# Attention queries kept in DRAM by chunk: one load a chunk, two stores a batch

## The chip, the cores and the metric

The kernel runs on one core of one Trainium2 chip. The metric is the device time of one execution in microseconds.

## What is computed

Two layers over x of shape (8, 512, 256), each an attention and a feed-forward block with a residual and a layer norm behind each. The change is in the attention of the second layer, which mixes the 16 heads of one token with each other, token by token:

```python
xn = _rms(x, g1)
Q, K, V = ...            # xn @ W.T, each (b, s, H=16, HD=16)
pQ, pK = elu(Q), elu(K)
Q1, Q2 = split(pQ, 2, axis=-1);  K1, K2 = split(pK, 2, axis=-1)
kv1 = einsum('bshe,bshd->bsed', K1, V) * SCALE
kv2 = einsum('bshe,bshd->bsed', K2, V) * SCALE
lmb = exp(lp[0] * lp[1]) - exp(lp[2] * lp[3]) + LAMBDA_INIT
attn = einsum('bshe,bsed->bshd', Q1, kv1) - lmb * einsum('bshe,bsed->bshd', Q2, kv2)
```

So components 0 to 7 of a head's query are scaled by SCALE and components 8 to 15 by -lmb * SCALE. Before that come the first layer (a retention block and a ternary feed-forward block), after it norms per head and per row, an MLP, routing, and eight experts.

## The kernel before

Everything is f32; the 4096 tokens are 32 tiles of 128. The kernel has three programs behind one another: first layer and projections, attention with MLP and routing, experts. In each, every engine runs its own list of instructions and waits on semaphores; SP issues nearly all DMAs from one list, in order.

**Projections** (end of the first program, `attention_inputs`). A batch is 512 tokens. For each of 8 batches the matmul engine transposes the normalised tokens (`front`, L1338) and makes six items: two of queries (L1365), two of keys and two of values (`interleaved`, L1349). ScalarE takes exp and relu of an item (L1297, L1298), VectorE joins them to an elu (L1418) and writes the result into `res[b % 2]`, queries with the scale `qscale` (L1424). `qscale` is a column that differs between the first and the second half of each group of 16 partitions, made by five small steps (L1433 to L1442) just before the first normalisation of this stage (L1403). SP stores each batch: the queries with one DMA (L1266), the keys and values with two each (L1270). Before VectorE writes `res[b % 2]` again, it waits on `stored[n][b % 2]`.

The query tensor in DRAM is (256 features, 4096 tokens), so a store moves rows of 512 tokens (2 KB). After batch 2 SP also issues the loads of chunk 0, after batch 4 the queries and keys of chunk 1.

**Attention** (`attention_mlp_and_route`). A unit is 8 tiles, a chunk m is one half (64 tokens) of each of the 8 tiles of a unit, and there are 8 chunks. The queries of a chunk are brought to 128 partitions (tile j times component e) with 16 heads and 64 tokens in each:

```python
for j in range(GROUPS):      # 8
    src = net.q_dram.rearrange("(h e) t -> e h t", e=HD)[:, :, first:first + HALF]
    sp.dma_start(net.q[m % 2][j * HD:(j + 1) * HD, :, :], src)
```

that is 8 DMAs of 64 KB in runs of 64 tokens (256 B). Keys and values go to a ring of three buffers, 8 DMAs each, with runs of 1 KB. The matmul engine runs rounds n of 16 columns each, four rounds a chunk: `scores(n)` (L1687), `mix(n - 2)` (L1710), `turn_scores(n - 1)` (L1696), `turn_mixes(n - 3)` (L1718), and in some rounds `turn_heads` (L1726). The first `scores` of a chunk waits for the queries (`q_in`) and the keys (`ring_in`), and each `scores` for a bank (`a_taken`); the first `mix` of a chunk waits for its values, each for `t_taken` (the copy at L2023). SP's list in this loop is, for each chunk m from 2 on: wait until the scores of chunk m - 2 are done (`a_made`), queries of m; wait until the mixes of chunk m - 2 are done (`o_made`), keys of m; wait until the scores of chunk m - 1 are done, values of m. VectorE makes the copies of each round and, between them, the norms of heads and rows (L2036 to L2087).

Of the kernel before, what the change touches and what calls it, by code (L numbers as in the profile page):

```python
# [6 lines left out]
F32 = mybir.dt.float32  # L7
# [8 lines left out]
P = 128  # L16
# [34 lines left out]
def constant_table(names, of_them):  # L51
# [25 lines left out]

    parts["firsthalf"] = (p % HD < HD // 2).astype(np.float64)[:, None]
    parts["sums"] = np.stack([(p // 32 % 2 == k) / (32.0 * HID) for k in range(2)], 1)
# [74 lines left out]
class Net:  # L154


    def __init__(self, nc, ctx, args):
# [11 lines left out]

        self.q_dram = nc.dram_tensor("q_dram", [DIM, TOKENS], F32).ap()  # L170
        self.kv_dram = nc.dram_tensor("kv_dram", [2, ROWS4, TOKENS * RUN], F32).ap()
# [1044 lines left out]

STORES = (16, 32, 32)


def attention_inputs(net, ctx):  # L1220
# [24 lines left out]

    res = [[spare[:, (3 * p + n) * KD * SEQ:(3 * p + n + 1) * KD * SEQ].rearrange("p (k t) -> p k t", k=KD) for n in range(3)] for p in two]
    bank = [ph.ps(f"bank{i}", [P, SEQ]) for i in range(8)]
    pE, pV, pX = [bank[i] for i in (1, 2, 0, 3)], bank[4:6], bank[6:8]
# [11 lines left out]
    def sync(sp):  # L1260
        for b in range(BATCH):
            for n in range(3):
                sp.wait_ge(item_ready.sem, item_ready.after(ITEMS * b + KD * (n + 1)))
                kept = stored[n][b % 2].sem
                if n == 0:
                    sp.dma_start(net.q_dram[:, b * SEQ:(b + 1) * SEQ].rearrange("(k p) t -> p k t", p=P), res[b % 2][0]).then_inc(kept, 16)  # L1266
                else:
                    tokens = net.kv_dram[n - 1, :, b * SEQ * RUN:(b + 1) * SEQ * RUN].rearrange("r (j h c) -> h r j c", j=KD, h=2)
                    for h in two:
                        sp.dma_start(tokens[h], res[b % 2][n][h * ROWS4:(h + 1) * ROWS4, :, :]).then_inc(kept, 16)  # L1270
            if b in (2, 4):

                for n in range(3):
                    for kept in stored[n]:
                        sp.wait_ge(kept.sem, kept.after(STORES[n] * b // 2))
            if b == 2:
                sp.wait_ge(net.ring_zeroed.sem, net.ring_zeroed.after(4 * RING))
                load_queries(net, sp, 0)
                load_keys(net, sp, 0)
                load_values(net, sp, 0)  # L1280
            if b == 4:
                load_queries(net, sp, 1)
                load_keys(net, sp, 1)
# [103 lines left out]
    def vector(dve):  # L1387
# [18 lines left out]
        def body(b, p, before, behind, between=None):  # L1406
            if behind:
                norm(b + 1, 1 - p)
            for n in range(ITEMS):
# [13 lines left out]
                if part == 0:  # L1423
                    ins = dve.tensor_scalar(to, rl[n % 2][:, :], 1.0, qscale[:, :], ALU.subtract, ALU.mult)  # L1424
                elif part == 1:
                    ins = dve.tensor_scalar(to, rl[n % 2][:, :], 1.0, None, ALU.subtract)
                else:
                    ins = dve.tensor_copy(to, pV[n - 4][:, :])
                ins.then_inc(item_ready.sem, 1)

        def first(last_norm):
            dve.wait_ge(exp_lam.sem, exp_lam.after(1))
            dve.tensor_tensor(lmb[:, 0:1], lmb[:, 2:3], lmb[:, 3:4], ALU.subtract).then_inc(steps.sem, 1)  # L1433
            dve.wait_ge(steps.sem, steps.done(1))
            dve.tensor_scalar(lmb[:, 0:1], lmb[:, 0:1], LAMBDA_INIT, 1.0, ALU.add, ALU.add).then_inc(steps.sem, 1)
            dve.wait_ge(steps.sem, steps.done(1))

            dve.tensor_scalar(lmb[:, 1:2], net.table["firsthalf"], lmb[:, 0:1], 1.0, ALU.mult, ALU.add).then_inc(steps.sem, 1)
            dve.wait_ge(steps.sem, steps.done(1))
            dve.tensor_tensor(lmb[:, 1:2], lmb[:, 1:2], lmb[:, 0:1], ALU.subtract).then_inc(steps.sem, 1)  # L1440
            dve.wait_ge(steps.sem, steps.done(1))
            dve.tensor_scalar(qscale[:, :], lmb[:, 1:2], RET_SCALE, None, ALU.mult).then_inc(steps.sem, 1)  # L1442
            dve.wait_ge(steps.sem, steps.done(1))
# [50 lines left out]
def load_queries(net, sp, m):  # L1494
    for j in range(GROUPS):
        first = (m // 2 * GROUPS + j) * P + m % 2 * HALF
        src = net.q_dram.rearrange("(h e) t -> e h t", e=HD)[:, :, first:first + HALF]
        sp.dma_start(net.q[m % 2][j * HD:(j + 1) * HD, :, :], src).then_inc(net.q_in[m % 2].sem, 16)

# [18 lines left out]
def attention_mlp_and_route(net, ctx):  # L1518
# [157 lines left out]
    def _(pe):  # L1676
        def scores(n):

            m = n // SETS
            if n % SETS == 0:  # L1680
                pe.wait_ge(net.q_in[m % 2].sem, net.q_in[m % 2].after(128 * (m // 2 + 1)))
                pe.wait_ge(net.ring_in[2 * m % RING].sem, net.ring_in[2 * m % RING].after(128 * (2 * m // RING + 1)))
# [1017 lines left out]
def laid_out(inputs):  # L2700
# [4 lines left out]
    wk = given("L1_attn_Wk").reshape(split, RUN, HD, DIM).transpose(1, 0, 2, 3).reshape(DIM, DIM)  # L2705
    wv = given("L1_attn_Wv").reshape(HD, split, RUN, DIM).transpose(2, 1, 0, 3).reshape(DIM, DIM)
    column = lambda v: v.reshape(-1, P).T
    every = lambda v: np.broadcast_to(v.reshape(1, -1), (P, v.size))
# [6 lines left out]
        "w_fcT": flat(given("L0_ffn_W_fc").T), "w_projT": flat(given("L0_ffn_W_proj").T),  # L2715
        "w_qkvT": by_rows(np.concatenate([given("L1_attn_Wq"), wk, wv], 0).T),
        "w_1T": by_rows(given("L1_attn_W1").T), "w_2T": by_rows(given("L1_attn_W2").T),
# [18 lines left out]
```

## Time and profile before

| | |
|---|---|
| median of 3 runs | 923.56 us (922.23 to 925.37) |
| span of the profiled execution | 923.6 us |
| granted TensorE clock, mean | 0.953 |
| DVE, ACT, POOL busy | 67%, 52%, 28% |
| q1 (the hardware queues of SP) | 71376 packets, 72.36 MB, 25.5% of 16 engines |
| packets under 512 B | 22592 |

The profile is of one execution; nothing that can be measured lies between its span and the time of the runs. Times in the rows are microseconds from the start of the span. Of a matmul row with a gap before it the bracket gives the idle time and what ended it; "issue" means that the profile shows no releaser. The projection stage lasts from about 412 to 515 us, the attention loop from 518 to 633 us. PEclk is the granted clock as a share of full speed.

### The profile page before, as it was taken

Reading aid. Unit: us, or ns where it says so; the run is one execution under the profiler, and the core shown is the slowest. Engines: PE = TensorE matmul, PEld = TensorE weight load, DVE = VectorE, ACT = ScalarE, POOL = GpSimd, SP = SyncE. Lnnn points to the kernel's source line nnn. Section 1 sums busy time; section 2 is a strip of 40 time slices with the busy share of each in tenths; the row PEclk is TensorE's granted clock in tenths of the full one; section 3 lists DMA queues with packets and bytes.
Section 4 is the critical chain, followed back from the end, with each engine's and each line's share of the span. In section 5 each row is a group of like instructions: output and inputs, shape, how many; then the busy total and the mean of one; then the engine's idle time right before and its main releaser. Section 6 shows DMA issues by size and latency. Waiting matters only on the chain. (4 is left out here: it accounts for less than half of the span.)

```text
span 923.6 us, 23206 instructions
## 1 busy us (share of the span) xinstructions
PE 826.7 (90%) x8838; PEld 688.1 (75%) x8838; DVE 614.9 (67%) x1408; ACT 481.8 (52%) x999; POOL 254.6 (28%) x323
## 2 busy tenths in 40 slices
PE   5999999998899999998999889889989839999960
PEld 4788888887677777766777778777667729999960
DVE  2578787878547777777565425677776875756626
ACT  2444444443777777766954324544654224445325
POOL 1156664221202222223000000004232131656344
PEclk9999999999999999999999989999989769999985
DMA  8500000000000000002476344435222212656439
GB/s 309 184 25 17 23 17 23 17 11 2 1 1 1 1 2 1 1 1 70 139 194 189 99 111 114 117 89 178 92 93 92 92 29 84 161 160 190 122 50 344
DMA packets 76429, 79.56 MB, mean 86 GB/s; under 512 B 22592, under 2 KB 66496, under 8 KB 75968
## 3 DMA queue, kind: packets, MB, share of 16 engines
q1 hardware_dynamic: 71376, 72.36, 25.5%
q0 software_dynamic: 3968, 5.25, 3.3%
q8 instruction: 50, 0.82, 0.4%
q10 hardware_dynamic: 1008, 0.91, 0.3%
q14 instruction: 27, 0.22, 0.1%
HBM read 50.71 MB, written 27.79 MB: 85 GB/s over the span
## 5 line engine op out<-in xcount | busy, mean ns | idle before, releaser
L713 DVE TENSOR_TENSOR r_prob<-r_pS,const 128x512 f32<-128x512 f32 x128 | 82.0, 682 | 25.1 <-PE r_pS L540 25.1
L1089 DVE SCALAR_TENSOR_TENSOR f_gl<-att_res,small_first,f_gh 128x512 fp32r<-128x512 f32 x64 | 47.3, 748 | 37.2 <-ACT f_gh L1014 34.7
L943 PE MATMUL f_pY<-wpjT,f_gh 128*128 128x256 f32 x256 | 66.1, 292 | 0.3 <-DVE f_gl L1089 0.3
L944 PE MATMUL f_pY<-wpjT,f_gl 128*128 128x256 f32 x256 | 63.4, 281 | 0.0
L1349 PEld LDWEIGHTS q_bank<-q_xT,att_res 128*64 128x64 f32 x1024 | 55.6, 137 | 7.2 <-issue 4.2
L943 PEld LDWEIGHTS f_pY<-wpjT,f_gh 128*128 128x128 f32 x256 | 48.7, 190 | 15.9 <-issue 13.4
L2426 POOL DMA_INDIRECT sum_dram<-e_yo,y_id x24 | 43.1, 1795 | 63.1 <-ACT e_yo L2559 47.4
L1349 PE MATMUL q_bank<-q_xT,att_res 128*64 128x128 f32 x1024 | 59.2, 274 | 0.0
L1008 ACT ACTIVATE att_res<-f_pH 128x512 f32<-128x512 f32 x64 | 38.0, 594 | 40.1 <-PE f_pH L928 39.4
L2540 ACT ACTIVATE e_hh<-e_pH 128x320 fp32r<-128x320 f32 x64 | 26.2, 433 | 55.3 <-PE e_pH L2465 55.0
L839 POOL TENSOR_SCALAR t_ey<-t_es 128x8 f32<-128x8 f32 x4 | 0.8, 202 | 195.0 <-ACT t_sqrow L1911 195.0
L928 PE MATMUL f_pH<-f_xh,wfcT 128*128 128x512 f32 x128 | 52.4, 409 | 0.0
L928 PE MATMUL f_pH<-f_xl,wfcT 128*128 128x512 f32 x128 | 51.1, 399 | 0.0
L944 PEld LDWEIGHTS f_pY<-wpjT,f_gl 128*128 128x128 f32 x256 | 48.7, 190 | 1.8
L1014 ACT ACTIVATE f_gh<-att_res,small_first 128x512 fp32r<-128x512 f32 x64 | 46.3, 723 | 2.1
L2599 DVE SCALAR_TENSOR_TENSOR e_hl<-e_pH,e_hh 128x320 fp32r<-128x320 f32 x64 | 28.5, 486 | 28.3 <-ACT e_hh L2540 28.3
L2023 DVE COPY t_scT<-t_pT 128x256 f32<-128x256 f32 x32 | 14.0, 438 | 48.1 <-PE t_pT L1696 47.0
L512 PE MATMUL r_pQV<-r_xT,w_first 128*128 128x128 f32 x256 | 37.2, 292 | 9.7 <-DMA r_xT<-xT 7.3
L1687 PE MATMUL t_pA<-t_ring,t_q 128*16 128x128 f32 x1024 | 36.7, 284 | 7.9 <-issue 4.5
L1418 DVE SCALAR_TENSOR_TENSOR q_rl<-q_ex,q_rl 128x512 f32<-128x512 f32 x32 | 22.1, 691 | 29.6 <-ACT q_rl L1298 29.3
L512 PEld LDWEIGHTS r_pQV<-r_xT,w_first 128*128 128x128 f32 x256 | 33.4, 204 | 10.8 <-DMA w_first<-w_qkv 7.2
L1710 PE MATMUL t_pO<-t_ring,t_scT 128*16 128x128 f32 x1024 | 36.0, 280 | 4.9 <-DVE t_scT L2023 4.8
(307 smaller groups left out, 2363.2 us busy)
## 6 DMA issues: line engine op xcount, KB each, us to landing
kv_dram<-att_res SPq DMA_DIRECT2D x32, 256.0 KB, 3.7
t_ring<-kv_dram SPq DMA_DIRECT2D x128, 64.0 KB, 2.3
wi<-L_ffn_wi SPq DMA_DIRECT2D x8, 1024.0 KB
wo<-L_ffn_wo SPq DMA_DIRECT2D x8, 1024.0 KB
x_res<-L_attn_x SPq DMA_DIRECT2D x8, 512.0 KB, 5.1
q_dram<-att_res SPq DMA_DIRECT2D x8, 512.0 KB, 3.1
t_q<-q_dram SPq DMA_DIRECT2D x64, 64.0 KB, 2.8
x_dram<-x_res SPq DMA_DIRECT2D x8, 512.0 KB, 3.0
```

The costliest lines, as they stand in the source:

```text
L512: pe.matmul(pQ[:, m, :], w[:, k, m * P:(m + 1) * P], xT[t][:, k, :], start=(k == 0), stop=(k == KD - 1))
L713: dve.tensor_tensor(prob[t % 2][:, r, :, :], pS[r][:, :, :], dec[:, r, :, :], ALU.mult)\
L928: mm = pe.matmul(pH[c % 2][:, :], net.wfcT[:, k, c * P:(c + 1) * P], part[b % 2][:, k, :], start=(k == 0 and part is xh), stop=(k == KD - ...
L943: pe.matmul(out, gh[c % 4][:, cols], net.wpjT[:, c, :], start=(c == 0 and t % 2 == 0), stop=False, skip_group_check=True)
L944: mm = pe.matmul(out, gl[c % 4][:, cols], net.wpjT[:, c, :], start=False, stop=(c == NH - 1), skip_group_check=True)
L1008: nc.scalar.activation(g[c][:, :], pH[c % 2][:, :], ACT.Gelu).then_inc(gelued.sem, 1)
L1014: nc.scalar.activation(gh[c % 4][:, :], g[c][:, :], ACT.Copy, scale=net.lnw[:, c:c + 1]).then_inc(high.sem, 1)
L1089: dve.scalar_tensor_tensor(out=gl[c % 4][:, :], in0=g[c][:, :], scalar=net.lnw[:, c:c + 1], in1=gh[c % 4][:, :], op0=ALU.mult, op1=ALU.sub ...
L1349: mm = pe.matmul(to, net.wqkvT[:, k, cols], xT[p][:, k, tile], start=(k == 0), stop=(k == KD - 1))
L1687: mm = pe.matmul(pA[n % 2][32 * c:32 * c + HEADS, g, :], net.q[m % 2][:, :, at], net.ring[2 * m % RING][:, :, at * RUN:(at + 1) * RUN], st ...
L1710: mm = pe.matmul(pO[n % 2][32 * c:32 * c + HEADS, g, :], scT[n % 2][:, 4 * g + c, :], net.ring[i % RING][:, :, at * RUN:(at + 1) * RUN], s ...
L2426: pool.indirect_dma_start(net.sum_dram[:, :], bass.IndirectOffsetOnAxis(ap=net.y_id[0:n, r, e:e + 1], axis=0), yo[e % 2][0:n, r, :], None, ...
```

## The change

The query tensor in DRAM becomes (8 chunks, 2048 rows, 64 tokens), the 2048 rows being (tile, component, head). A chunk is then one block of 512 KB in which each partition of the loaded tile has one run of 4 KB, and one DMA loads it. The rows of the query weights are reordered on the host to (component, head), so that the first item of the projection holds components 0 to 7 of all heads and the second 8 to 15. The scale becomes a constant for the first and one value (-lmb * SCALE on every partition) for the second item, which takes three steps out of its making. VectorE writes the queries as (tile, item, token), 128 tokens a run. A store of a batch's queries becomes two DMAs, one for each half of the tiles, with runs of 64 tokens (256 B). `STORES` and the count that the matmul engine waits for follow.

```diff
--- before.py
+++ after.py
@@ -75,7 +75,6 @@
 
     parts["first"] = np.tile(EXPERTS - np.arange(EXPERTS), (P, 1))
 
-    parts["firsthalf"] = (p % HD < HD // 2).astype(np.float64)[:, None]
     parts["sums"] = np.stack([(p // 32 % 2 == k) / (32.0 * HID) for k in range(2)], 1)
     parts["rmseps"] = np.full((P, 1), RMS_EPS)
     parts["minushalf"] = np.full((P, HEADS), -0.5)
@@ -167,7 +166,7 @@
         self.w2T = self.sb("w2T", [P, KD, DIM])
 
 
-        self.q_dram = nc.dram_tensor("q_dram", [DIM, TOKENS], F32).ap()
+        self.q_dram = nc.dram_tensor("q_dram", [2 * UNITS, GROUPS * DIM, HALF], F32).ap()
         self.kv_dram = nc.dram_tensor("kv_dram", [2, ROWS4, TOKENS * RUN], F32).ap()
         self.x_dram = nc.dram_tensor("x_dram", [TOKENS, DIM], F32).ap()
         self.sum_dram = nc.dram_tensor("sum_dram", [TOKENS, DIM], F32).ap()
@@ -1214,7 +1213,7 @@
 
 
 
-STORES = (16, 32, 32)
+STORES = (32, 32, 32)
 
 
 def attention_inputs(net, ctx):
@@ -1244,6 +1243,11 @@
     rl = [ph.sb(f"rl{i}", [P, SEQ]) for i in two]
 
     res = [[spare[:, (3 * p + n) * KD * SEQ:(3 * p + n + 1) * KD * SEQ].rearrange("p (k t) -> p k t", k=KD) for n in range(3)] for p in two]
+
+    def queries_of(p):
+
+        return res[p][0].rearrange("p k t -> p (k t)").rearrange("p (a t) -> p a t", t=P)
+
     bank = [ph.ps(f"bank{i}", [P, SEQ]) for i in range(8)]
     pE, pV, pX = [bank[i] for i in (1, 2, 0, 3)], bank[4:6], bank[6:8]
     lam_ready, exp_lam = (ph.sig(n) for n in ("lam_ready", "exp_lam"))
@@ -1263,7 +1267,10 @@
                 sp.wait_ge(item_ready.sem, item_ready.after(ITEMS * b + KD * (n + 1)))
                 kept = stored[n][b % 2].sem
                 if n == 0:
-                    sp.dma_start(net.q_dram[:, b * SEQ:(b + 1) * SEQ].rearrange("(k p) t -> p k t", p=P), res[b % 2][0]).then_inc(kept, 16)
+                    tiles = queries_of(b % 2)
+                    for half in two:
+                        rows = net.q_dram[b // 2 * 2 + half].rearrange("(b a p) t -> b p a t", b=2, p=P)[b % 2]
+                        sp.dma_start(rows, tiles[:, :, half * HALF:(half + 1) * HALF]).then_inc(kept, 16)
                 else:
                     tokens = net.kv_dram[n - 1, :, b * SEQ * RUN:(b + 1) * SEQ * RUN].rearrange("r (j h c) -> h r j c", j=KD, h=2)
                     for h in two:
@@ -1421,7 +1428,9 @@
                 else:
                     dve.wait_ge(v_made.sem, v_made.after(2 * b + n - 4 + 1))
                 if part == 0:
-                    ins = dve.tensor_scalar(to, rl[n % 2][:, :], 1.0, qscale[:, :], ALU.subtract, ALU.mult)
+                    to = queries_of(p).rearrange("p (t k) c -> p t k c", k=KD)[:, :, n, :]
+                    elu = rl[n % 2][:, :].rearrange("p (t c) -> p t c", c=P)
+                    ins = dve.tensor_scalar(to, elu, 1.0, qscale[:, :] if n else RET_SCALE, ALU.subtract, ALU.mult)
                 elif part == 1:
                     ins = dve.tensor_scalar(to, rl[n % 2][:, :], 1.0, None, ALU.subtract)
                 else:
@@ -1432,14 +1441,7 @@
             dve.wait_ge(exp_lam.sem, exp_lam.after(1))
             dve.tensor_tensor(lmb[:, 0:1], lmb[:, 2:3], lmb[:, 3:4], ALU.subtract).then_inc(steps.sem, 1)
             dve.wait_ge(steps.sem, steps.done(1))
-            dve.tensor_scalar(lmb[:, 0:1], lmb[:, 0:1], LAMBDA_INIT, 1.0, ALU.add, ALU.add).then_inc(steps.sem, 1)
-            dve.wait_ge(steps.sem, steps.done(1))
-
-            dve.tensor_scalar(lmb[:, 1:2], net.table["firsthalf"], lmb[:, 0:1], 1.0, ALU.mult, ALU.add).then_inc(steps.sem, 1)
-            dve.wait_ge(steps.sem, steps.done(1))
-            dve.tensor_tensor(lmb[:, 1:2], lmb[:, 1:2], lmb[:, 0:1], ALU.subtract).then_inc(steps.sem, 1)
-            dve.wait_ge(steps.sem, steps.done(1))
-            dve.tensor_scalar(qscale[:, :], lmb[:, 1:2], RET_SCALE, None, ALU.mult).then_inc(steps.sem, 1)
+            dve.tensor_scalar(qscale[:, :], lmb[:, 0:1], LAMBDA_INIT, -RET_SCALE, ALU.add, ALU.mult).then_inc(steps.sem, 1)
             dve.wait_ge(steps.sem, steps.done(1))
             batches(dve, body, steps, 4, first=last_norm)
 
@@ -1492,10 +1494,8 @@
 
 
 def load_queries(net, sp, m):
-    for j in range(GROUPS):
-        first = (m // 2 * GROUPS + j) * P + m % 2 * HALF
-        src = net.q_dram.rearrange("(h e) t -> e h t", e=HD)[:, :, first:first + HALF]
-        sp.dma_start(net.q[m % 2][j * HD:(j + 1) * HD, :, :], src).then_inc(net.q_in[m % 2].sem, 16)
+    src = net.q_dram[m].rearrange("(p h) t -> p h t", h=HEADS)
+    sp.dma_start(net.q[m % 2][:, :, :], src).then_inc(net.q_in[m % 2].sem, 16)
 
 
 def load_diagonal(net, sp, part, m, i):
@@ -1678,7 +1678,7 @@
 
             m = n // SETS
             if n % SETS == 0:
-                pe.wait_ge(net.q_in[m % 2].sem, net.q_in[m % 2].after(128 * (m // 2 + 1)))
+                pe.wait_ge(net.q_in[m % 2].sem, net.q_in[m % 2].after(16 * (m // 2 + 1)))
                 pe.wait_ge(net.ring_in[2 * m % RING].sem, net.ring_in[2 * m % RING].after(128 * (2 * m // RING + 1)))
             pe.wait_ge(a_taken.sem, a_taken.after(n - 1))
             for g in range(4):
@@ -2704,6 +2704,7 @@
     split = HEADS // RUN
     wk = given("L1_attn_Wk").reshape(split, RUN, HD, DIM).transpose(1, 0, 2, 3).reshape(DIM, DIM)
     wv = given("L1_attn_Wv").reshape(HD, split, RUN, DIM).transpose(2, 1, 0, 3).reshape(DIM, DIM)
+    wq = given("L1_attn_Wq").reshape(HEADS, HD, DIM).transpose(1, 0, 2).reshape(DIM, DIM)
     column = lambda v: v.reshape(-1, P).T
     every = lambda v: np.broadcast_to(v.reshape(1, -1), (P, v.size))
     by_head = lambda v: np.repeat(v.reshape(KD, HPK).T, HD, 0)
@@ -2713,7 +2714,7 @@
         "xT": x.reshape(TILES, P, KD, P).transpose(0, 3, 2, 1),
         "w_qkv": by_rows(given("L0_attn_W_qkv")),
         "w_fcT": flat(given("L0_ffn_W_fc").T), "w_projT": flat(given("L0_ffn_W_proj").T),
-        "w_qkvT": by_rows(np.concatenate([given("L1_attn_Wq"), wk, wv], 0).T),
+        "w_qkvT": by_rows(np.concatenate([wq, wk, wv], 0).T),
         "w_1T": by_rows(given("L1_attn_W1").T), "w_2T": by_rows(given("L1_attn_W2").T),
         "small": np.concatenate([column(given("L1_attn_g1")), every(given("L1_attn_lambda_params")), flat(given("L1_ffn_w_router")),
                                  every(given("L1_attn_g2")), every(given("L1_attn_g3"))], 1),
```

## Rows read from the trace of the kernel before

**Rows 1.** The page: busy time of each engine, and one group of instructions.
```profile
PE 826.7 (90%) x8838; PEld 688.1 (75%) x8838; DVE 614.9 (67%) x1408; ACT 481.8 (52%) x999; POOL 254.6 (28%) x323
...
L1418 DVE SCALAR_TENSOR_TENSOR q_rl<-q_ex,q_rl 128x512 f32<-128x512 f32 x32 | 22.1, 691 | 29.6 <-ACT q_rl L1298 29.3
```

**Rows 2.** The page: DMA issues, count, KB each, median us to landing.
```profile
kv_dram<-att_res SPq DMA_DIRECT2D x32, 256.0 KB, 3.7
t_ring<-kv_dram SPq DMA_DIRECT2D x128, 64.0 KB, 2.3
...
q_dram<-att_res SPq DMA_DIRECT2D x8, 512.0 KB, 3.1
t_q<-q_dram SPq DMA_DIRECT2D x64, 64.0 KB, 2.8
```

**Rows 3.** Timeline of TensorE, attention loop: start, us, instruction, idle before it.
```profile
529.14 1.12 PE L1687 MATMUL t_pA<-t_ring,t_q 128*16 128x128 f32 x32
530.06 1.08 PE L1710 MATMUL t_pO<-t_ring,t_scT 128*16 128x128 f32 x32
...
535.08 1.12 PE L1687 MATMUL t_pA<-t_ring,t_q 128*16 128x128 f32 x32
...
541.21 1.95 PE L1687 MATMUL t_pA<-t_ring,t_q 128*16 128x128 f32 x32 [3.11 <-issue]
...
546.69 1.20 PE L1687 MATMUL t_pA<-t_ring,t_q 128*16 128x128 f32 x32
...
569.77 1.12 PE L1687 MATMUL t_pA<-t_ring,t_q 128*16 128x128 f32 x32 [0.51 <-issue]
...
598.34 1.13 PE L1687 MATMUL t_pA<-t_ring,t_q 128*16 128x128 f32 x32 [0.89 <-issue]
...
611.36 1.54 PE L1710 MATMUL t_pO<-t_ring,t_scT 128*16 128x128 f32 x32 [3.06 <-DVE t_scT L2023]
```

**Rows 4.** Timeline of SP's DMA queue: start, us of issuing, instruction, count.
```profile
427.14 0.39 SPq L1266 DMA_DIRECT2D q_dram<-att_res  x1
...
529.43 4.90 SPq L1498 DMA_DIRECT2D t_q<-q_dram  x8
534.38 8.61 SPq L1507 DMA_DIRECT2D t_ring<-kv_dram  x16
...
548.81 8.90 SPq L1507 DMA_DIRECT2D t_ring<-kv_dram  x16
557.96 4.88 SPq L1498 DMA_DIRECT2D t_q<-q_dram  x8
...
586.98 4.44 SPq L1498 DMA_DIRECT2D t_q<-q_dram  x8
591.46 9.95 SPq L1507 DMA_DIRECT2D t_ring<-kv_dram  x16
```

**Rows 5.** Windows: busy us by engine, granted clock, DMA share, GB/s.
```profile
498.00:510.00 12.00, 12.00 (x150) 9.30 (x148) 6.04 (x11) 5.59 (x11) 0.00 (x0) 1.00 0.48 141
524.40:529.40 5.00, 5.00 (x120) 4.24 (x112) 1.58 (x4) 2.39 (x4) 0.00 (x0) 1.00 0.32 83
529.43:534.30 4.87, 4.87 (x138) 4.28 (x129) 1.55 (x3) 1.93 (x4) 0.00 (x0) 1.00 0.44 103
541.20:543.00 1.80, 1.79 (x36) 1.80 (x40) 0.00 (x0) 0.00 (x0) 0.00 (x0) 0.50 0.48 138
```

**Rows 6.** Timeline of VectorE, projection stage.
```profile
423.10 0.21 DVE L1438 TENSOR_SCALAR q_lmb<-const,q_lmb 128x1 f32<-128x1 f32 x1
...
423.73 1.14 DVE L1403 TENSOR_SCALAR q_xn<-x_res,q_rs 128x256 f32<-128x256 f32 x4
...
438.37 0.49 DVE L1424 TENSOR_SCALAR att_res<-q_rl,q_qscale 128x512 f32<-128x512 f32 x1
...
507.93 0.49 DVE L1424 TENSOR_SCALAR att_res<-q_rl,q_qscale 128x512 f32<-128x512 f32 x1
```

**Rows 7.** Timeline of TensorE, projection stage.
```profile
424.93 1.09 PE L1338 MATMUL q_bank<-const,q_xn 128*128 128x128 f32 x8 [2.74 <-DVE q_xn L1403]
```

## The prediction, made before the changed kernel was run

> **What bounds the kernel now.** I read the page's busy shares first: the matmul engine is busy 90% of the span [rows 1], so what the change can give back must be idle time of that engine, or work at its lower clock, on the way to the end. Second, the page's DMA issues: 64 loads `t_q<-q_dram` of 64 KB beside 128 of the key and value ring, and 8 stores of queries [rows 2]. Third, the timeline of the matmul engine over the attention loop (518 to 631 us): it runs without a gap except at a few starts of a round. Those at 541.21, 569.77 and 598.34 begin with `scores` of chunks 2, 4 and 6 and are put down to "issue", that is to nothing the profile names; `scores` waits there only for the chunk's queries and keys and for `a_taken`. The other large one (611.36, 3.06 us) waits for VectorE's copy at L2023 and has nothing to do with loads [rows 3].
>
> Fourth, SP's queue in the same stretch. It works without rest: 8 query loads take 4.4 to 4.9 us of issuing, 16 ring loads 8.6 to 10 us [rows 4], some 13.5 to 15 us a chunk, where four rounds of the matmul engine at 2.97 us (529.14 to 535.08 is two) take 11.9. Take chunk 2. Its keys may be issued when `mix(3)` is done, at 530.06 + 1.08 = 531.14, but SP is then still issuing queries (529.43 to 534.33) and starts the keys at 534.38. Eight of them take half of 8.61, 4.3 us, and land 2.3 us later [rows 2, 4]: 541.0. The matmul engine, free at 535.08 + 2.97 = 538.05, starts at 541.21. This identifies the releaser that the profile leaves open. Chunk 3 is the counter-example: its keys start at 548.81, right where `mix(7)` ends (about 2.0 us into the round that starts at 546.69), so the queue is not late, and no gap stands before its scores.
>
> **The change, part by part.**
>
> *One query load for eight.* SP loses 7 issues a chunk: 4.90 us becomes one of about 0.61 (4.90/8), bounds 0.4 (the store at 427.14) and 0.61. For chunk 2 SP then sits ready at 530.1 and the keys start at the gate, 531.2, instead of 534.38. They land at 531.2 + 4.3 + 2.3 = 537.8, just before 538.05. So the stall of 3.11 goes; with the slowest ring issue seen (9.95/2 = 5.0) they would land at 538.5 and leave 0.5. Chunks 4 and 6 lose 0.51 and 0.89 in the same way, since queries there occupy SP for 4.88 and 4.44 us before the keys [rows 3, 4]. What is late next: the gate `o_made` itself, then the ring loads behind it, with about 0.2 us of slack. I charge 0.2 us in all for that, and keep 0 and 1.5 (three chunks times 0.5) as bounds. Values come earlier too, and nobody waited for them.
>
> *The clock.* The stall at 541 costs more than its length. In the stretch from 541.2 the granted clock is 0.50, the 1.2 GHz level, against 1.00 before it, after an idle of 3.11 us [rows 5]. That round takes 546.69 - 541.21 = 5.48 us instead of 2.97: 2.51 us. The idles of 0.51 and 0.89 have no slow round behind them. With the stall gone I take back all 2.51; bounds 0 (the clock falls at another place instead) and 2.5 plus the similar slow round after 611.36, about 1.6, if that stall, too, becomes shorter. I take none of the latter: head normalisation at L2036 to L2073 occupies VectorE whatever the loads do.
>
> *Transfer of the load.* It is still 512 KB, now in 4 KB runs rather than 256 B ones, and is issued at the same gate a round ahead of the keys. It has about 8 us to land before chunk 2's scores; the 512 KB store of [rows 2] needs 3.1. No cost.
>
> *Two stores of 256 B runs per batch.* Runs go from 512 tokens (2 KB, 256 of them) to 64 tokens (256 B, 2048 of them): 128 packets for each of the 16 DMA engines per batch where there were 16. No store in the trace has such packets, so I bound their cost. From below: the old query loads have exactly this size; 128 packets an engine kept them 0.44 x 4.87 = 2.14 us busy, 17 ns each. The 1 KB ring loads took 0.32 x 5.0 / 32 = 50 ns each. From above: a 2 KB store packet; a batch's stores (1.69 MB in the window, 52 packets an engine) took 0.48 x 12 = 5.8 us, 112 ns each [rows 5]. Size governs reads; a write into DRAM may be worse, so I take 30 ns, nearest the row of equal size: 3.8 us a batch, beside 32 x 0.112 = 3.6 for keys and values. That is 7.4 us of DMA in a batch of 12.0 us in which the matmul engine is busy for 12.00 of 12.00 us (498 to 510). Hidden.
>
> The Trainium skill ("DMA: Bandwidth & Descriptors", Specifications) speaks against this part: transfers under 512 B make the DMA engine read, modify and write, so they miss line rate. If that doubled the 17 ns of the equal-sized read, the store would take 4.4 us a batch, and the sum would be the same; the trace has no small write to confirm either.
>
> Who waits for the stores: VectorE, which reuses the result tile two batches later (24 us), and SP ahead of chunk loads; both have slack at 30 ns. The second issue costs SP 0.4 to 0.6 us a batch; only the key and value stores stand behind it, and their takers are two batches away as well.
>
> *VectorE.* The lambda chain loses three dependent steps. Before, its third step starts at 423.10 and the normalisation at 423.73; now the latter can start at 423.10: 0.63 us. The matmul engine had waited 2.74 us for that normalisation (424.93) [rows 6, 7], so the first rounds behind it move forward whole: 0.63. The rest of this stage is a chain of PE and ACT work that moves with it. The strided result of the 16 query writes (L1424) keeps 512 elements in rows of 128; I take its 0.49 us as unchanged. If it fell to the 0.69 of the 128x512 operation L1418 [rows 1, 6], 16 x 0.20 = 3.2 us would be the most it could cost, and most would be hidden behind the matmul engine. Reordered weight rows are made on the host and change no instruction.
>
> **Sum.** 3.11 + 0.51 + 0.89 + 2.51 + 0.63 - 0.2 = 7.45 us. The span of the profiled execution is 923.6, equal to the median of the runs (923.56), so the forecast is 916.2 us.
>
> **Rivals.**
>
> A. *Partial gain.* The stall shrinks, but about 1.5 us of it stays at the gate in the three chunks, or the clock drops at another pause. For it: the slack of 0.2 us is thin. Against it: chunk 3, already at its gate, has no gap. Without the clock 4.9 us are left; without both 3.5: 918.7 to 920.1 us.
>
> B. *Nothing comes through.* The freed time is absorbed before the end by VectorE: head and row normalisation already holds the matmul engine for 3.06 us at 611.36, and a faster loop would simply wait longer there. For it: VectorE's rest between copies is about 1 us in those rounds. Against it: that work is released by the same rounds and so moves with them. Only the 0.63 and some clock would be left: 922 to 923.5 us, within 0.3%, which is about what a measurement of this kernel can tell from no change.
>
> C. *Slower: the small stores become the bound of the projection stage.* Mechanism: if a 256 B write costs what a 2 KB one does, 112 ns, the query store takes 14.3 us of every DMA engine, and with 3.6 for keys and values 17.9 us a batch against 12.0. VectorE's first query write of batch 7 (507.93) waits until batch 5's store is through. Stores begin at about 427; chunk loads share the rings (three ring loads of 1.6 us and two query loads of about 2: 9 us). That gives 427 + 5 x 17.9 + 14.3 + 3 + 9 = 543, or 35 us late; less the 7.45 gained, 951 us. It begins to show when 427 + 5 x (128t + 3.6) + 128t + 12 passes 508, at t = 66 ns, and outweighs the gain at t = 76 ns. For it: nothing in the trace shows a small write, so the 2 KB row stands as its upper bound. Against it: the equal-sized read is at 17 ns and t has to be over four times as much. (The Trainium skill's rule on transfers under 512 B, named above, points this way.)
>
> **How the numbers follow.** The forecast 0.60 (914 to 918.5), A 0.18, B 0.09, C 0.13. The likeliest value is 916.2. The range has to leave out no more than 2 in 10: I leave out C and most of B, and reach down by the 1.6 us of clock after 611.36 and a little more: 913.5 to 921. Faster by over 0.3% (under 920.8) is the forecast and nearly all of A: 0.77. Within 0.3%: B and the edge of A, 0.11. Slower: C, with 0.12.
>
> **What the changed profile would show.** No idle of over 0.6 us ahead of `scores` of chunks 2, 4 and 6, and no slow round behind chunk 2; one `t_q` issue a chunk on SP and SP waiting for `mix` before the keys; attention loop about 6.8 us shorter, its start 0.6 us earlier; the stall of about 3 us at VectorE's normalisation still there. DMA share in a projection batch about 0.6 with the matmul engine still busy all of it; query stores that land in 4 to 8 us. Wrong it would be if `stored` waits appear on VectorE (C), if the clock falls elsewhere (A), or if the pause at L2023 grows by what the chunk starts lose (B).

## The result, and the profile after

The changed kernel takes 918.22 us (median of 11 runs, 912.71 to 920.96) against 924.27 for the kernel before in the same comparison: ratio 0.9934, 95% interval 0.9919 to 0.9950, or 6.1 us less (4.6 to 7.5). The forecast was 7.45 us less. The profiled execution has a span of 916.7 us where the one before had 923.6. One run of the kernel before in a later comparison took 3699 us and is left out of every mean below.

The page's DMA issues of the changed kernel answer to [rows 2]:

```profile
kv_dram<-att_res SPq DMA_DIRECT2D x32, 256.0 KB, 3.3
t_ring<-kv_dram SPq DMA_DIRECT2D x128, 64.0 KB, 2.3
...
q_dram<-att_res SPq DMA_DIRECT2D x16, 256.0 KB, 3.4
t_q<-q_dram SPq DMA_DIRECT2D x8, 512.0 KB, 3.8
```

One query load a chunk now, of 512 KB, landing in 3.8 us; two stores a batch of 256 KB each, landing in 3.4, hardly later than the single 512 KB store of 2 KB runs did (3.1).

SP's queue in the attention loop (start, us of issuing, count), beside [rows 4]:

```profile
530.68 0.34 SPq L1498 DMA_DIRECT2D t_q<-q_dram  x1
532.75 9.89 SPq L1507 DMA_DIRECT2D t_ring<-kv_dram  x16
...
554.94 0.34 SPq L1498 DMA_DIRECT2D t_q<-q_dram  x1
558.28 10.55 SPq L1507 DMA_DIRECT2D t_ring<-kv_dram  x16
```

The query load of chunk 2 takes SP 0.34 us, not 4.90. After it SP waits for its gate until 532.75, so the query loads are no longer what makes the keys late. The matmul engine around the start of chunk 2, beside [rows 3]:

```profile
536.60 1.13 PE L1687 MATMUL t_pA<-t_ring,t_q 128*16 128x128 f32 x32
...
540.62 1.13 PE L1687 MATMUL t_pA<-t_ring,t_q 128*16 128x128 f32 x32 [0.99 <-issue]
...
543.58 1.12 PE L1687 MATMUL t_pA<-t_ring,t_q 128*16 128x128 f32 x32
```

The idle is 0.99 us where it was 3.11, and no slow round follows: 543.58 - 540.62 = 2.96 us where it was 5.48. At chunks 4 and 6 there is no idle at all. The 0.99 us is the keys' own: their eight issues took SP 4.85 us from 532.75 where the prediction took 4.3, and one of them landed 3.6 us after its issue, not 2.3. The pause at L2023 is still there, 2.91 us; this time the matmuls behind it run at full speed (2.46 us to the next scores, against 615.43 - 611.36 = 4.07). The first line is of the kernel before, the others of the changed one:

```profile
615.43 1.13 PE L1687 MATMUL t_pA<-t_ring,t_q 128*16 128x128 f32 x32
```

```profile
606.40 1.07 PE L1710 MATMUL t_pO<-t_ring,t_scT 128*16 128x128 f32 x32 [2.91 <-DVE t_scT L2023]
...
608.86 1.12 PE L1687 MATMUL t_pA<-t_ring,t_q 128*16 128x128 f32 x32
```

But the loop begins slowly. The first 64 score matmuls take 3.66 us, and the four rounds of chunk 0 take 10.53 us, where before they took 2.01 and 7.98 (526.18 - 518.20). First the two lines of the kernel before, then the changed kernel from the projections to the end of chunk 0, then its windows (busy us by engine, granted clock, DMA share, GB/s):

```profile
518.20 2.01 PE L1687 MATMUL t_pA<-t_ring,t_q 128*16 128x128 f32 x64 [3.37 <-DVE t_pA L2102]
...
526.18 1.14 PE L1687 MATMUL t_pA<-t_ring,t_q 128*16 128x128 f32 x32
```

```profile
424.16 1.09 PE L1345 MATMUL q_bank<-const,q_xn 128*128 128x128 f32 x8 [2.08 <-DVE q_xn L1410]
...
517.21 3.66 PE L1687 MATMUL t_pA<-t_ring,t_q 128*16 128x128 f32 x64 [3.37 <-DVE t_pA L2102]
...
527.74 1.15 PE L1687 MATMUL t_pA<-t_ring,t_q 128*16 128x128 f32 x32
```

```profile
497.00:509.00 12.00, 12.00 (x150) 9.30 (x148) 5.98 (x11) 5.60 (x11) 0.00 (x0) 1.00 0.53 131
517.00:521.00 4.00, 3.79 (x65) 3.02 (x66) 1.68 (x5) 0.73 (x2) 0.00 (x0) 0.50 0.23 78
```

The granted clock is 0.50 (1.2 GHz) in 517 to 521, behind an idle of 3.37 us that the kernel before has as well, followed there by full speed in its profile. So 2.52 us (5.48 - 2.96) came back at chunk 2, about 1.6 behind L2023, and 2.55 were lost at chunk 0. From its first scores to those of its last round the loop is 5.6 us shorter, not 6.8. The window of a projection batch has a DMA share of 0.53 (in the kernel before 0.46 in a window that moved the same bytes, below) and the matmul engine busy for 12.00 of 12.00 us: the small stores are hidden.

A window of a batch in the kernel before (same columns):

```profile
499.00:511.00 12.00, 12.00 (x150) 9.30 (x148) 5.97 (x11) 5.54 (x10) 0.00 (x0) 1.00 0.46 132
```

VectorE's scale chain and two query writes of a batch, beside [rows 6, 7]:

```profile
422.77 0.15 DVE L1444 TENSOR_SCALAR q_qscale<-q_lmb 128x1 f32<-128x1 f32 x1
422.96 1.14 DVE L1410 TENSOR_SCALAR q_xn<-x_res,q_rs 128x256 f32<-128x256 f32 x4
...
437.55 0.43 DVE L1433 TENSOR_SCALAR att_res<-q_rl 128x512 f32<-128x512 f32 x1
...
438.61 0.49 DVE L1433 TENSOR_SCALAR att_res<-q_rl,q_qscale 128x512 f32<-128x512 f32 x1
```

The normalisation starts 0.77 us earlier, and the transposes behind it (424.16 against 424.93) as well. The strided write costs what the plain one did, 0.49 us, and 0.43 with a constant for a scale. The latter brings another 0.06 us at the first query write of each of the first four batches, so the loop starts 0.99 us earlier (517.21 against 518.20).

Of these starts about 0.1 us is not the change's. This stage begins at another time in every execution: the transposes start anywhere from 421.1 to 424.9 us in the thirteen profiles. What does not vary is their wait ahead of the first transposes, 2.73 or 2.74 us in the three kernels with the long chain of before and 2.08 to 2.10 in the nine with the short one, and the time from there to the first scores, 93.27 to 93.29 against 93.01 to 93.05 us (stores_x4 apart). That makes 0.65 + 0.24 = 0.9 us for the change.

The loop starts when SP is through with its stores. The last ones of the first program, of the kernel before and of the changed one:

```profile
513.68 3.15 SPq L1270 DMA_DIRECT2D kv_dram<-att_res  x4
```

```profile
512.69 3.14 SPq L1277 DMA_DIRECT2D kv_dram<-att_res  x4
```

They end at 516.83 and 515.83, and the first scores follow 1.37 and 1.38 us later; in all thirteen profiles it is 1.36 to 1.38.

### The profile page after: what moved, and what is told of

It is laid out like the page before. It is cut to its first block and busy times, and to the rows that moved or that the text cites. A ratio compares the mean times of both kernels' runs of the same rounds, so it can differ in the third digit from the quotient of the medians.

```text
span 916.7 us, 23149 instructions
## 1 busy us (share of the span) xinstructions
PE 824.3 (90%) x8838; PEld 685.8 (75%) x8838; DVE 613.7 (67%) x1405; ACT 482.3 (53%) x999; POOL 254.7 (28%) x323
## 5 line engine op out<-in xcount | busy, mean ns | idle before, releaser
L2023 DVE COPY t_scT<-t_pT 128x256 f32<-128x256 f32 x32 | 14.1, 442 | 43.6 <-PE t_pT L1696 40.3
L433 ACT ACTIVATE att_res<-r_pRR 128x256 f32<-128x256 f32 x32 | 12.3, 384 | 53.5 <-PE r_pRR L580 52.7
```

## The experiments

Ratios are against the kernel before, on the same chip. Over all comparisons, the changed kernel ran 17 times (mean 918.1 us) and the kernel before 74 times with a recorded clock (mean 923.7): 5.6 us, with a standard error of 0.6. The mean of the granted clocks is 0.955 for both, with a standard error of 0.001 for the changed kernel.

**Eight loads of the new layout.** The changed kernel with its query load cut into eight.

```diff
-    sp.dma_start(net.q[m % 2][:, :, :], src).then_inc(net.q_in[m % 2].sem, 16)
+    for j in range(GROUPS):
+        rows = slice(j * HD, (j + 1) * HD)
+        sp.dma_start(net.q[m % 2][rows, :, :], src[rows]).then_inc(net.q_in[m % 2].sem, 16)
```

> The changed kernel with its one query load split again into eight of 64 KB, each 16 partitions with 4 KB runs. If SP's issuing is what made the keys late, SP is again busy for 4.4 to 4.9 us a chunk ahead of the keys, the idle ahead of the scores of chunk 2 is again 2.5 to 3.5 us, chunks 4 and 6 have 0.3 to 1 us, and the time is 4 to 7 us above the changed kernel, near the kernel before less its 0.8 us in the lambda chain. If instead the size of the packets did it, the time stays within 1 us of the changed kernel and no idle over 1 us stands there.

Measured: 921.70 us (12 runs, mean 922.1), ratio 0.9982 (0.9962 to 1.0001): 4.0 us above the mean of the changed kernel (standard error 0.8). SP's queue and the matmul engine in its profile:

```profile
530.25 4.44 SPq L1500 DMA_DIRECT2D t_q<-q_dram  x8
534.73 8.31 SPq L1509 DMA_DIRECT2D t_ring<-kv_dram  x16
```

```profile
541.07 1.13 PE L1689 MATMUL t_pA<-t_ring,t_q 128*16 128x128 f32 x32 [1.98 <-issue]
...
554.31 1.13 PE L1689 MATMUL t_pA<-t_ring,t_q 128*16 128x128 f32 x32 [0.93 <-issue]
```

SP is again busy for 4.44 us ahead of the keys, although each run is now 4 KB, and the idles are back: 1.98 us at chunk 2 and 0.93 at chunk 3. They are shorter and stand at other chunks than before. At chunk 2 SP came to the keys 9.27 us after it had begun the values of chunk 1 (525.46 to 534.73), where before it took 9.99 (524.39 to 534.38). At chunk 3 the prediction had found no idle and called it the counter-example; but there `mix(7)` came late, behind the idle of 3.11 us and the slow round. Here no slow round follows, `mix(7)` is done at 546.0, and SP is busy with query loads until 547.8: this queue was late for chunk 3 as well. Four of the 5.6 us hang on the number of issues alone.

**Whole tiles.** Queries in DRAM as (unit, row, 128 tokens): one store a batch with runs of 512 B, one load a chunk with 2048 runs of 256 B.

```diff
-        self.q_dram = nc.dram_tensor("q_dram", [2 * UNITS, GROUPS * DIM, HALF], F32).ap()
+        self.q_dram = nc.dram_tensor("q_dram", [UNITS, GROUPS * DIM, P], F32).ap()
...
+                    rows = net.q_dram[b // 2].rearrange("(b a p) t -> b p a t", b=2, p=P)[b % 2]
+                    sp.dma_start(rows, tiles).then_inc(kept, 16)
...
+    src = net.q_dram[m // 2].rearrange("(p h) t -> p h t", h=HEADS)[:, :, m % 2 * HALF:(m % 2 + 1) * HALF]
```

> The changed kernel with queries kept in DRAM by whole tile: one store a batch with runs of 512 B, and still one load a chunk, but of 2048 runs of 256 B. If the number of issues is what counts, the time is that of the changed kernel within 1 us, and t_q takes 0.3 to 0.6 us of SP a chunk. If small packets of the load count, the load lands late and the idle ahead of the scores of chunk 2 grows above 2 us: 2 to 5 us slower than the changed kernel. The DMA share of a projection batch of 12 us should fall from 0.53 to about 0.48.

Measured: 918.59 us, ratio 0.9938 (0.9919 to 0.9958), the changed kernel's. Its matmul engine at chunks 2 and 3, and the window of a projection batch:

```profile
536.58 1.13 PE L1686 MATMUL t_pA<-t_ring,t_q 128*16 128x128 f32 x32 [0.99 <-issue]
...
549.18 1.12 PE L1686 MATMUL t_pA<-t_ring,t_q 128*16 128x128 f32 x32 [0.29 <-issue]
```

```profile
494.00:506.00 12.00, 12.00 (x150) 9.30 (x148) 5.97 (x11) 5.59 (x11) 0.00 (x0) 1.00 0.49 131
```

The same 0.99 us at chunk 2 and 0.29 at chunk 3: one issue with small packets is as good as one with large ones. With eight_loads this is the other half of the proof, fewer issues and not larger packets. The DMA share is 0.49, where 0.48 was expected.

**Stores four times.** Every query store made four times, three of them to tensors nobody reads.

```diff
-                    for half in two:
...
+                    for q_dram in (net.q_dram, *net.q_more):
+                        for half in two:
...
-STORES = (32, 32, 32)
+STORES = (128, 32, 32)
```

> The changed kernel with each query store made four times, three of them to tensors that nobody reads. Measured by the DMA share, a 256 B packet of a store took (0.53 - 0.46) x 12 us more than the 2 KB ones it replaced, some 21 ns each, 2.7 us a batch. Four times that and 3.7 us for keys and values are 14.4 us against a batch of 12: the stores become the bound, VectorE waits for the result tile, and the time is 8 to 20 us above the changed kernel. If the DMA share overstates or the buffers of two batches cover it, the time is unchanged within 2 us; if small writes are dearer than read off, over 25 us are added.

Measured: 948.80 us, ratio 1.0271 (1.0233 to 1.0309), 31 us above the changed kernel, where 8 to 20 were expected. Windows of its projection stage, the wait of VectorE on a store (us in all, times, longest), SP's last batch, and the matmul engine's first scores:

```profile
487.00:500.00 13.00, 12.61 (x156) 9.74 (x155) 6.22 (x14) 5.50 (x10) 0.00 (x0) 1.00 0.96 231
519.00:532.70 13.70, 0.00 (x0) 0.00 (x0) 4.85 (x9) 2.17 (x4) 0.00 (x0) 0.50 0.97 234
```

```profile
DVE q_rl L1427 <- DMA q_more<-att_res: 24.3, 3, 12.1
```

```profile
519.15 2.34 SPq L1275 DMA_DIRECT2D q_dram<-att_res  x2
...
532.80 2.36 SPq L1275 DMA_DIRECT2D q_dram<-att_res  x2
535.20 6.91 SPq L1275 DMA_DIRECT2D q_more<-att_res  x6
542.15 3.92 SPq L1279 DMA_DIRECT2D kv_dram<-att_res  x4
```

```profile
547.45 3.67 PE L1689 MATMUL t_pA<-t_ring,t_q 128*16 128x128 f32 x64 [31.80 <-DVE t_pA L2104]
```

The DMA engines are busy 0.96 to 0.97 of the time, and SP starts a batch of stores every 13.7 us (519.15 in its list, then 532.80), so the price of a packet can be read at saturation: 13.7 x 0.97 = 13.3 us, less 32 x 0.112 = 3.6 for keys and values, over 4 x 128 packets is 19 ns. In the changed kernel the share rose by 0.07 of 12 us in place of 16 packets of 112 ns: (0.84 + 1.79) / 128 = 21 ns. The trace's own packet records agree: in the projection stage the 256 B packets have a mean of 18 ns in either kernel. So the write was not dearer than read off. What was wrong was the place at which it decides. VectorE does wait 24.3 us for its tile, but the loop does not start when VectorE is done: SP has to issue its last store first (546.07), since the next program begins only when every engine has left the one before; the first scores follow 1.38 us later, as in every profile. With the DMA engines at 0.97 an issue took SP 1.15 us (6 in 6.91), where it took 0.79 in the changed kernel (4 in 3.14). So all eight batches count.

**Three steps back in the chain.**

```diff
+            for _ in range(3):
+                dve.wait_ge(steps.sem, steps.done(1))
+                dve.tensor_scalar(lmb[:, 1:2], qscale[:, :], 1.0, None, ALU.mult).then_inc(steps.sem, 1)
```

> The changed kernel with three dependent single-column VectorE steps put back behind the scale of the queries, as many as the change took out. If the chain is on the path that sets the end, the matmul engine's transposes behind it start 0.6 to 0.8 us later and the whole kernel takes 0.5 to 0.9 us more, which five rounds can barely tell; the attention loop starts that much later in the profile. If the work behind it waits for something else, nothing moves in the profile.

Measured: 916.28 us (6 runs), ratio 0.9918 (0.9885 to 0.9950); the time can't tell the effect. The profile can:

```profile
424.75 1.09 PE L1345 MATMUL q_bank<-const,q_xn 128*128 128x128 f32 x8 [2.65 <-DVE q_xn L1410]
...
517.77 2.01 PE L1690 MATMUL t_pA<-t_ring,t_q 128*16 128x128 f32 x64 [3.37 <-DVE t_pA L2105]
```

The transposes start 0.59 us later than in the changed kernel and the scores 0.56 us later, and the wait ahead of the transposes is longer by as much (2.65 against 2.08): the chain is on the path and worth what was forecast. By chance this execution has no slow stretch at all in the loop, and with full speed from the start (2.01 us for the first 64) its span is 913.2 us, although it has more work.

**The kernel before and the changed one again**, unchanged, for second profiles.

> The kernel before itself, once more. Expected: the idles ahead of the scores of chunks 2, 4 and 6 again (about 3, 0.5 and 0.9 us), since they come from SP's queue. If the slow round behind chunk 2 (5.48 us) is a consequence of the idle of 3.11 us it comes again; if it is a matter of the execution it may be absent, and then this profile is about 2.5 us shorter. Ratio of times 1.000 within its interval.

Measured: ratio 1.0003 (0.9987 to 1.0019). Its matmul engine at chunk 0, chunk 2 and the round behind it:

```profile
518.17 2.59 PE L1687 MATMUL t_pA<-t_ring,t_q 128*16 128x128 f32 x64 [3.37 <-DVE t_pA L2102]
...
542.67 1.45 PE L1687 MATMUL t_pA<-t_ring,t_q 128*16 128x128 f32 x32 [3.14 <-issue]
...
547.23 1.12 PE L1687 MATMUL t_pA<-t_ring,t_q 128*16 128x128 f32 x32
```

The idle at chunk 2 is 3.14 us again, and the round behind it slow again, though 4.56 us long and not 5.48. But at chunk 4, where 0.5 us was expected again, there is no idle, and at chunk 6 it is 0.34 us and not 0.89: the small ones vary from one execution to the next. Now chunk 0 is slow as well (2.59), and it was not in the first profile.

> The changed kernel itself, once more, for its profile and its time beside the others. If the slow first rounds of the attention loop (3.66 us for the first 64 score matmuls instead of 2.01, granted clock 0.50) belong to the kernel, they come again; if they are a matter of the execution, they may be absent, and then the loop is 2 to 2.6 us shorter. The idle ahead of the scores of chunk 2 is expected again, 0 to 1 us.

Measured: 919.71 us, ratio 0.9949 (0.9931 to 0.9968). Chunk 0 and chunk 2:

```profile
515.63 3.65 PE L1687 MATMUL t_pA<-t_ring,t_q 128*16 128x128 f32 x64 [3.37 <-DVE t_pA L2102]
...
537.90 1.13 PE L1687 MATMUL t_pA<-t_ring,t_q 128*16 128x128 f32 x32
```

Slow at chunk 0 again (3.65), no idle at chunk 2 (no bracket at 537.90), and slow behind L2023, where the first profile was not. The pause at L2023 is thus followed by a slow stretch or not, from one execution of the kernel to the next; for the idle of 3.37 us ahead of chunk 0 the other kernels show the same (last section).

**Half of the keys on ScalarE.** The changed kernel with four of the eight key loads of a chunk issued by ScalarE behind `take_mixes`.

```diff
-                load_keys(net, sp, m)
+                load_keys(net, sp, m, range(GROUPS // 2))
...
+            m = (n - 1) // SETS + 1
+            if (n - 1) % SETS == 0 and 2 <= m < CHUNKS:
+                load_keys(net, nc.scalar, m, range(GROUPS // 2, GROUPS))
```

> The changed kernel with four of the eight key loads of chunks 2 to 7 issued by ScalarE behind its copy of the same mixes, so that both queues issue at once. If the keys' own issuing behind the mix gate (4.3 to 5 us) and landing (2.3) is what leaves 0.99 us ahead of the scores of chunk 2, that idle goes and the time falls 0.5 to 1.5 us. If ScalarE's issuing (some 2 us a chunk) delays its copies of scores and mixes, the matmul engine gets new waits on them and the time rises by 1 to 5 us.

Measured: 916.08 us (6 runs), ratio 0.9915 (0.9888 to 0.9943). No idle at a chunk's start in its profile, and none on ScalarE's account. The interval overlaps that of the changed kernel, and its mean clock was higher (0.9585 against 0.955), so a further gain is not shown.

**The kernel before with its keys on ScalarE.** Nothing else changed: eight small query loads, old stores.

```diff
-                sp.wait_ge(o_made.sem, o_made.after(SETS * (m - 1)))
-                load_keys(net, sp, m)
...
+            m = (n - 1) // SETS + 1
+            if (n - 1) % SETS == 0 and 2 <= m < CHUNKS:
+                load_keys(net, nc.scalar, m)
```

> The kernel before, with its eight small query loads and its stores as they were, and only the eight key loads of chunks 2 to 7 moved from SP to ScalarE, behind its copy of the same mixes. If the whole gain of the change in the loop is that the keys no longer queue behind query loads on SP, this gets it as well: no idle over 1 us ahead of the scores of chunks 2, 4, 6, and 3 to 7 us faster than before, without any change to transfers or stores. If the gain came from the larger packets, nothing is gained; if 4 us of issuing a chunk on ScalarE delays its copies, it is slower than the kernel before.

Measured: 919.83 us, ratio 0.9965 (0.9949 to 0.9980), 3.2 us faster than before (1.8 to 4.7).

SP's queue ahead of the keys of chunk 2, in its profile:

```profile
528.88 5.52 SPq L1498 DMA_DIRECT2D t_q<-q_dram  x8
```

Its matmul engine at chunk 2:

```profile
540.03 1.13 PE L1685 MATMUL t_pA<-t_ring,t_q 128*16 128x128 f32 x32 [1.88 <-issue]
```

With 5.52 us of query issues still on SP, the idle at chunk 2 falls from 3.1 to 1.88 us, and those at 4 and 6 go. What remains fits ScalarE's own issuing: its eight key loads start at 530.86, with its copy of the mixes, but take 5.39 us to issue and up to 4.1 us more to land. They also make the matmul engine wait 0.29 us for a copy of scores. So 3.2 of the 5.6 us come without any new layout: the queue in front of the keys was the cause.

**The query load on ScalarE**, some 5 us ahead of the keys, to see whether the transfer of 512 KB just ahead of them makes the remaining idle.

```diff
-                load_queries(net, sp, m)
...
+            if (n + 1) % SETS == 0 and 2 <= (n + 1) // SETS + 1 < CHUNKS:
+                m = (n + 1) // SETS + 1
+                ...
+                load_queries(net, nc.scalar, m)
```

> The changed kernel with the one query load of chunks 2 to 7 issued by ScalarE right behind its copy of the scores that free the buffer, some 4 to 5 us before SP came to it. If the 512 KB query load just ahead of the keys is what makes their issuing and landing long (one key issue took 1.68 us, one landing 3.6 us in the changed kernel), the keys land in 2.1 to 2.6 us, no idle stands ahead of the scores of chunk 2, and the time is 0 to 1 us below the changed kernel. If the last 1 us of idle is a chance of landing, an idle of up to 1 us still appears.

Measured: 918.27 us, ratio 0.9946 (0.9923 to 0.9968).

The matmul engine at chunk 2, in its profile:

```profile
540.48 1.13 PE L1686 MATMUL t_pA<-t_ring,t_q 128*16 128x128 f32 x32 [1.10 <-issue]
```

Ten ring loads on SP between 529.3 and 537.5 us, of which the eight from 532.5 to 537.1 are the keys: time of issuing in ns (least, median, most), and from issue to landing in us (likewise):

```profile
L1507 SPq DMA_DIRECT2D t_ring<-kv_dram x10: 311/426/1799, 529.3 to 537.5; - x10
...
DMA to landing us min/median/max: 2.2/2.6/4.2
```

The idle is 1.10 us: the query load in front was not its cause. Of the eight keys one landed only 3.6 us after its issue (the 4.2 is of another load), and one issue took 1.80 us; in after_again, without an idle, it was at most 2.9 and 1.14. With the 0.2 us of slack that the prediction worked out such a landing shows at once. Why single ring loads land late stays open.

> Queries in DRAM by whole tile (one store a batch with 512 B runs, one load a chunk with 256 B runs) and the query load on ScalarE. Expected: the time of the changed kernel or up to 1.5 us below it, 916 to 919 us, with no idle over 0.5 us ahead of the scores of chunk 2. If loads of 256 B packets disturb the keys, an idle of 0.3 to 1 us remains at chunks 2 and 3.

Measured, both edits together: 917.46 us, ratio 0.9940 (0.9921 to 0.9958), with no idle ahead of chunk 2. No version is shown to be faster than the changed kernel.

**Keys made late at chunk 2 alone**, by cutting that one query load into ten.

```diff
+    cuts = [0, 8, 16, 24, 32, 48, 64, 80, 96, 112, P] if m == 2 else [0, P]
+    for rows in (slice(a, b) for a, b in zip(cuts, cuts[1:])):
+        sp.dma_start(net.q[m % 2][rows, :, :], src[rows]).then_inc(net.q_in[m % 2].sem, 16)
```

> The changed kernel with the query load of chunk 2 alone cut into ten DMAs, so that its keys are issued some 3 us behind their gate. If an idle of about 3 us ahead of chunk 2 brings a slow round with it, as in both profiles of the kernel before, the profile shows an idle of 2.5 to 3.6 us and behind it 3 to 5 us at a granted clock of 0.50, the mean clock of the runs falls by 0.002 to 0.003, and the kernel takes 4 to 6 us more than the changed one. If the clock's slow stretches are only moved from one place to another, the mean clock is unchanged and it takes 2.5 to 3.6 us more, the idle alone.

Measured: 922.65 us (mean 922.3), ratio 0.9991 (0.9973 to 1.0009), 4.1 us above the mean of the changed kernel (standard error 0.8); mean clock 0.9543 against 0.9551 (standard error of the difference 0.0012).

The matmul engine at chunk 2 and the round behind it, in its profile:

```profile
539.14 1.96 PE L1689 MATMUL t_pA<-t_ring,t_q 128*16 128x128 f32 x32 [3.60 <-issue]
...
543.66 1.12 PE L1689 MATMUL t_pA<-t_ring,t_q 128*16 128x128 f32 x32
```

An idle of 3.60 us, and a slow round of 4.52 us behind it, 1.57 too long. The idle accounts for 3.0 of the 4.1 us (3.60, from this one profile, less the 0.6 that kernels with one load have there on average), which leaves 1.1 for the clock. The slow round comes with the idle, so the first of the two expectations has its profile; but with an error of 0.8 us the times don't decide between them, and the mean clock, which fell by 0.0008, doesn't either. Whether part of the slow round is given back elsewhere is not shown.

## Why the prediction came out as it did

- **The releaser behind "issue" and the main stall: right.** 3.11, 0.51 and 0.89 us were SP's query issues. With one load a chunk the idles at chunks 4 and 6 are gone, chunk 2 has 0 to 1.1 us; eight_loads brings idles back, late_keys makes 3.60 us, and before_act_keys removes most without touching a transfer. Two readings were too neat: the eight query loads took SP 3.9 to 6.2 us over the six chunks and not 4.4 to 4.9, and chunk 3 was no counter-example (eight_loads).
- **The charge of 0.2 us for the gate behind: too small**, though within the 1.5 kept for three chunks. In the seven profiles of kernels with one load a chunk and all keys on SP (the changed one twice, whole_tiles, long_chain, act_query, whole_act_query, stores_x4) the idle ahead of chunk 2 was 0 three times and 0.91 to 1.10 us four times, 0.6 on average. The upper end that the prediction drew for one chunk from issuing alone was 0.5; it left out the spread of landings.
- **The clock, 2.51 us: the term that was mis-sized.** Its mechanism stands: in both profiles of the kernel before and in late_keys the round behind an idle of over 3 us is slow (5.48, 4.56, 4.52 us), and in none of the others, with 0 to 2 us of idle. But one profile's 5.48 was taken as a constant, and the other long idles were left as they were found. They change from execution to execution: at chunk 0 the four rounds took 7.98 and 9.50 us before, 10.53 and 10.45 after. Nor did the mean granted clock move: 2.51 us regained from the 1.2 GHz level are some 5 us less at 0.50, which in 920 us would raise the mean by 0.0027; it rose by 0.0001, with a standard error of 0.001. late_keys puts the average worth of the clock at about 1.1 us, with an error of 0.8.
- **The scale chain, 0.63: right** (0.65 less wait ahead of the transposes, 0.59 in long_chain), with 0.24 more from the constant scale, which had been charged at nothing.
- **The sum again**, with the means of the two profiles of the kernel before: 3.12 + 0.26 + 0.62 of idle, less 0.6, and 0.9 ahead of the loop make 4.3 us. The difference over all runs is 5.6 (standard error 0.6), which leaves 1.3 for the clock, beside the 1.1 of late_keys. Both errors are wide, so the clock term is smaller than 2.51 and not measured more closely. That the two first profiles differ by 6.9 us, near the forecast, is partly luck: 2.55 us of clock lost at chunk 0 stand against 1.6 won behind L2023, and the sum held neither.
- **The base.** The prediction set the span equal to the time of a run. The later runs show some 1.6 us around the span (918.34 against 916.7), so the profiled execution of before took about 925.2 us and was no typical one. Of the 2.1 us between forecast and result 0.7 are the base (923.6 against 924.27 in the comparison) and 1.4 the gain (7.45 against 6.05 between the medians).
- **Small stores, taken at 30 ns: cheaper.** 21 ns by the share, 19 at saturation, near the row of equal-sized reads (17) and far from the 2 KB row (112). Rival C fell with that. But its point of decision was misplaced: the end of the first program waits for SP, and so all eight batches count. On the prediction's own numbers 427 + 8 x (128t + 3.6) + 9 passes 516.8, where SP issued its last store before (513.68 + 3.15), from t = 51 ns, not 66. The rule in the Trainium skill ("DMA: Bandwidth & Descriptors", Specifications) that transfers under 512 B are read, modified and written did not show as a second pass: twice the 17 ns read would have been 34, and the 256 B store packets (18.2 ns in the packet records) are cheaper than the 512 B ones of whole_tiles (28.6), which the rule leaves out.
- **Rival A** (part of the stall stays) is what happened to some degree; **B** fell: VectorE's pause at L2023 stayed at 2.9 us and did not grow.

## What to carry to other kernels

Where the profile puts a gap down to "issue" at an instruction that waits for DMAs, lay the issuing queue's own timeline beside the gate of the transfer: a DMA mostly cost its queue 0.3 to 0.8 us here whether it carried 64, 256 or 512 KB (single ones up to 1.8), and what stands in front of the urgent one is the stall. Count such issues before packet sizes, and ask what starts only when the queue that issues the stores is done. A clock penalty seen once is a sample and not a term: look at a second profile, or at the mean clock of all runs, before it goes into a sum.

## What was not expected of the hardware

- After idles of 2.9 to 3.6 us of the matmul engine the granted clock fell to 0.50 in some executions and not in others of the same kernel: after 3.37 us at the loop's start the first 64 score matmuls took 2.01 or 2.59 us (before), 3.66 or 3.65 (after), 2.01 (long_chain, whole_act_query). The idles of over 3 us at chunk 2 were followed by a slow round in all three profiles that have one. After idles of 2.0 us or less in the loop it did so once in thirteen profiles (eight_loads, behind 1.73 us at L2025, where a transpose group took 1.12 us instead of 0.66).
- A 256 B packet of a store cost 19 to 21 ns of a DMA engine beside 112 ns for a 2 KB one, so cutting runs by eight cost the engines up to half as much again and not eight times.
- The Trainium skill ("DMA: Bandwidth & Descriptors", Issuing engines are not separate DMA queues) calls the time of issuing usually small beside the transfer. Here it was the larger: 3.9 to 6.2 us of SP for query loads that kept the engines busy 2.14 us in the window of [rows 5] (4.90 us of SP).
